# A two-expert feed-forward layer: the last batch's second layer by halves of the columns, its rows combined per half, and the sums of pieces on VectorE in that batch

## What is computed

```python
def _L0_ffn_ref(x, G, gate_w, up_w, down_w, lora_A, lora_B):   # x: the mask
    scores = softmax(einsum('bsh,he->bse', x, G))
    value, indices = top_k(scores, 2)
    w = einsum('bsk,bske->bse', value, onehot(indices))
    gate = silu(einsum('bsh,efh->bsef', x, gate_w))
    up = einsum('bsh,efh->bsef', x, up_w)
    out = einsum('bsef,bse,ehf->bsh', gate * up, w, down_w)
    lr = einsum('bsh,erh->bser', x, lora_A)
    return out + einsum('bser,bse,ehr->bsh', lr, w, lora_B)

return x + ffn
```

## Time and profile before

| | |
|---|---|
| median of 3 runs | 799.74 us (798.53 to 800.81) |
| the profiled execution: its own time | 801.34 us |
| the profiled execution: span from first to last instruction | 799.6 us |
| busy: TensorE matmul / VectorE / ScalarE / GpSimd | 500.2 / 518.0 / 450.5 / 386.0 us |
| chain that ended last: DMA / TensorE / VectorE / issue / GpSimd / ScalarE | 20 / 18 / 17 / 16 / 15 / 7% |
| moved by DMA | 147.29 MB, mean 184 GB/s |

### The profile page before, as it was taken

The page is one execution under the profiler, slowest core; times in us unless marked ns, Lnnn a source line. Parts: engine busy times, 40 slices in busy tenths (PEclk is TensorE's granted clock), DMA queues, the critical chain, the costliest instruction groups (busy, mean ns, idle before and its releaser), DMA issues.

```text
span 799.6 us, 13619 instructions
## 1 busy us (share of the span) xinstructions
PE 500.2 (63%) x3682; PEld 330.5 (41%) x3682; DVE 518.0 (65%) x1242; ACT 450.5 (56%) x655; POOL 386.0 (48%) x337
## 2 busy tenths in 40 slices
PE   0211187259878882687778716887779368888810
PEld 0210086136545551455445414554447155555500
DVE  5768789856697685776884867746872723233345
ACT  6687278837954576297446653875447245455410
POOL 7114200034365223387887224877973168768510
PEclk9755589668999995899999967989989779999965
DMA  9990060012312463368367823585479238758469
GB/s 317 360 270 0 4 260 27 1 40 98 128 71 103 146 238 102 119 227 287 132 222 227 349 94 130 181 274 183 158 251 361 86 107 293 248 179 283 174 259 381
DMA packets 76984, 147.29 MB, mean 184 GB/s; under 512 B 21475, under 2 KB 30699, under 8 KB 76400
## 3 DMA queue, kind: packets, MB, share of 16 engines
q1 hardware_dynamic: 59248, 104.40, 38.6%
q0 software_dynamic: 17664, 41.98, 14.3%
HBM read 95.47 MB, written 69.21 MB: 206 GB/s over the span
## 4 chain that ended last, share of the span: by engine, by line
DMA 20%; PE 18%; DVE 17%; issue 16%; POOL 15%; ACT 7%; DVEq 4%; SPq 3%; POOLq 1%; ACTq 0%
DMA piece<-put_rows 7%; DMA out_dram<-piece 6%; PE pa L692 6%; POOL piece L540 4%; ACT mask L807 3%; DMA xg<-mask_rows,where 3%; POOL piece L543 3%; DVE mask L1077 3%; POOL xg L523 2%; DMA w<-put_rows 2%; POOL put_rows L531 2%; DVE small L1039 1%; PE pc L718 1%; PE pc L715 1%; PE pc L717 1%
## 5 line engine op out<-in xcount | busy, mean ns | idle before, releaser
L692 PE MATMUL pa<-w,xt 128*128 x1472 | 204.1, 293 | 4.3 <-issue 4.2
L692 PEld LDWEIGHTS pa<-w,xt 128*128 128x128 f16 x1472 | 148.5, 101 | 67.2 <-issue 18.7
L864 ACT ACTIVATE y<-pc,where 128x512 f32<-128x512 f32 x184 | 125.5, 689 | 69.2 <-PE pc L718 69.0
L523 POOL DMA_INDIRECT xg<-mask_rows,where x92 | 97.2, 1056 | 119.4 <-DVEq L1351 93.8
L531 POOL DMA_INDIRECT put_rows<-y,where x92 | 92.4, 1005 | 127.7 <-ACT y L864 109.5
L1359 DVE SCALAR_TENSOR_TENSOR g_full<-pa,where,s_act 128x144 f32<-128x144 f32 x92 | 33.4, 364 | 176.3 <-ACT s_act L856 176.2
L851 ACT ACTIVATE xt<-pb 128x1024 f16<-128x1024 uint8 x92 | 94.1, 1023 | 92.4 <-PE pb L679 92.3
L856 ACT ACTIVATE s_act<-pa,small 128x128 f32<-128x128 f32 x92 | 33.9, 368 | 99.0 <-PE pa L692 99.0
L679 PE MATMUL pb<-ident,xg 128*128 128x128 f16 x368 | 38.6, 232 | 77.5 <-DMA xg<-mask_rows,where 59.1
L718 PE MATMUL pc<-lb,gt 128*128 x184 | 76.4, 415 | 0.0
L715 PE MATMUL pc<-wd,gt 128*128 x184 | 76.2, 414 | 0.3
(11 more groups left out here) (208 smaller groups left out, 863.4 us busy)
## 6 DMA issues: line engine op xcount, KB each, us to landing
piece<-put_rows SPq DMA_DIRECT2D x96, 256.0 KB, 3.9
v<-in_x_dram SPq DMA_DIRECT2D x40, 512.0 KB, 8.7
piece<-in_x_dram SPq DMA_DIRECT2D x48, 256.0 KB, 2.9
out_dram<-piece SPq DMA_DIRECT2D x48, 256.0 KB
w<-put_rows SPq DMA_DIRECT2D x16, 512.0 KB, 9.7
w<-in_L_ffn_gate_w_dram SPq DMA_DIRECT2D x8, 512.0 KB, 10.3
w<-in_L_ffn_up_w_dram SPq DMA_DIRECT2D x8, 512.0 KB, 8.3
wd<-in_L_ffn_down_w_dram SPq DMA_DIRECT2D x8, 512.0 KB, 9.5
```

The lines of the kernel that those rows point to most:

```text
L523: pool.indirect_dma_start(out=xg[:, g % NX, :], out_offset=None, in_=mask_rows[n % 2], in_offset=bass.IndirectOffsetOnAxis(ap=mask_row[n][ ...
L692: last = pe.matmul(l1[g % 2], xt[:, g % 2, t, :], w1[:, bass.ds(e, 1), t, k, :].rearrange("p o n -> p (o n)"), start=(t == 0 and k == 0), ...
L864: nc.scalar.activation(y[:, g % NY, half * HALF:(half + 1) * HALF], pc[:, half, :], ACT.Copy, scale=y_scale[n][:, i:i + 1]).then_inc(y_rea ...
```

## The change

In the last batch alone (`n == LAST`):

- The second layer runs by halves of the output columns. `half_layer(i, 0, e)` takes the place of `second_layer` in the loop over tiles; when the loop is over, `half_layer(i, 1, e)` runs for all 23 tiles, with the expert's number read again. So that the turned gates of all tiles stay, `store_gt` writes them to 23 buffers `late_gt`, 21 of them in the mask's memory and 2 in `gt`.
- ScalarE evicts a half as a unit of its own (`store_half`); the memory of `y` holds a ring of six halves. GpSimd puts each half (2 KB a row, up to 256 KB) with an indirect DMA of its own (`put_half`) into one of two new DRAM arrays `half_rows`: 46 puts in place of 23.
- SyncE waits for the puts of the first half, loads its 16 blocks of 256 KB, stores its 8 sums of 256 KB, and then does the same for the second half. VectorE adds by halves.
- The pieces of the batch before are added on VectorE, behind `store_gt` in the tile, and no longer on GpSimd.

Core of the diff:

```diff
+            def put_half(i, h):
+                u = late(h, i)
+                pool.wait_ge(y_ready, 2 * T * LAST + u + 1)
+                pool.indirect_dma_start(
+                    out=half_rows[h], out_offset=bass.IndirectOffsetOnAxis(ap=put_row[LAST][:, i:i + 1], axis=0),
+                    in_=late_y(u), in_offset=None,
+                    bounds_check=ROLES * S - 1, oob_is_err=False).then_inc(late_put[u % RING], 16)
...
-                    if i >= 3:
+                    if i >= 3 and n < LAST:
                         put_out(n, i - 3)
+                    elif i >= 3:
+                        put_half(i - 3, 0)
...
-                    if n > 0 and i in PIECE_AT:
+                    if 0 < n < LAST and i in PIECE_AT:
                         sum_piece(n - 1, PIECE_AT[i])
...
+            for i in range(T):
+                put_half(i, 1)
...
+            def half_layer(i, h, e):
+                u = late(h, i)
+                cols = slice(h * HALF, (h + 1) * HALF)
+                pe.wait_ge(gt_ready, tile(LAST, i) + 1)
+                pe.wait_ge(y_ready, 2 * T * LAST + u - 1)
...
+            for i in range(T):
+                half_layer(i, 1, load_expert(LAST, i))
...
+            def store_half(i, h):
+                u = late(h, i)
+                act.wait_ge(y_done, 2 * T * LAST + u + 1)
+                if u < RING:
+                    act.wait_ge(put[u // 2], 16 * len(range(u // 2, T * LAST, NY)))
+                else:
+                    act.wait_ge(late_put[u % RING], 16 * (u // RING))
...
+            def sum_piece(n, j):
+                u = PIECES * n + j
+                at = u % NC
+                dve.wait_ge(piece_landed[at], 48 * (u // NC + 1))
+                V.tensor_tensor(piece[:, at, 0, :], piece[:, at, 0, :], piece[:, at, 1, :], ALU.add)
+                dve.drain()
+                V.tensor_tensor(piece[:, at, 0, :], piece[:, at, 0, :], piece[:, at, 2, :],
+                                ALU.add).then_inc(summed_piece, 1)
...
+            for h in range(2):
+                cols = slice(h * HALF, (h + 1) * HALF)
+                for k in range(RING):
+                    sp.wait_ge(late_put[k], 16 * len(range(k, late(h, T), RING)))
+                for c in range(C):
+                    for r in range(ROLES):
+                        sp.dma_start(last_put[c][r][:, cols], half_roles[h][r][:, c, :]).then_inc(rows_landed[c], 16)
+                for c in range(C):
+                    sp.wait_ge(last_summed, C * h + c + 1)
+                    sp.dma_start(out_rows[n][:, c, cols], v[:, c, cols]).then_inc(last_stored, 16)
```

More of the change, by code:

```diff
@@ L214, in build @@
         expert_f = temp(T)
+        gt_cells = 3 * P
+        late_gt = [mask[:, k * gt_cells:(k + 1) * gt_cells].rearrange("p (t k) -> p t k", t=3)
+                   for k in range(NV // gt_cells)]
+        late_gt += [gt[:, i, :, :] for i in range(2)]
+        assert len(late_gt) >= T
         cells = [0]
@@ L306, in build @@
         put = [sem(f"put{i}") for i in range(NY)]
+        late_put = [sem(f"late_put{i}") for i in range(2 * NY)]
         piece_landed = [sem(f"piece_landed{i}") for i in range(NC)]
@@ L319, in build, with late, late_y @@
         out_rows = out.rearrange("b (p c) h -> b p c h", c=C)
+        half_rows = [nc.dram_tensor(f"half_rows{h}", [ROLES * S, HALF], F32, kind="Internal").ap()
+                     for h in range(2)]
+        half_roles = [a.rearrange("(r p c) h -> r p c h", r=ROLES, c=C) for a in half_rows]
+        LAST = B - 1
+        RING = 2 * NY
+        def late(half, i):
+            return T * half + i
+        def late_y(u):
+            return y[:, (u % RING) // 2, (u % 2) * HALF:(u % 2 + 1) * HALF]
         put_roles = [a.rearrange("(r p c) h -> r p c h", r=ROLES, c=C) for a in put_rows]
@@ L780, in _ @@
                     between(i, 2)
-                    if i >= 2:
+                    if i >= 2 and more:
                         second_layer(n, i - 2, experts[i - 2])
+                    elif i >= 2:
+                        half_layer(i - 2, 0, experts[i - 2])
                     between(i, 3)
@@ L940, in _ @@
                         exponential(n + 2, c)
+            for i in range(T - 2, T):
+                store_half(i, 0)
+            for i in range(T):
+                store_half(i, 1)
         @block.vector
@@ L1455, in _ @@
                     between(i, 2)
+                    if n == LAST and i in PIECE_AT:
+                        sum_piece(n - 1, PIECE_AT[i])
                 store_gt(n, T - 1)
```

71 lines of the change are left out of this document (44 added, 27 removed).

## The result

The changed kernel takes 814.62 us (median of 4 runs, 810.23 to 816.65) where the kernel before, on the same chip, takes 799.13 (4 runs, 794.29 to 800.81). The ratio is 1.0207, 95% interval 1.0167 to 1.0247: slower by 2.1%, where 0.9% was forecast and 814.0 was the range's upper end. The profiled execution took 815.52 us, its span is 813.8.

The account below looks back on a forecast made before the run. Last batch bound by waits in its 23-tile loop (piece cycle delaying gathers) and a transfer tail. Loop gains 12.5 us, puts cost 30.8, shorter tail gives 801.7, queueing adds 5.5: span 807.2, median 807.3 us; range 795 to 814.

Parts of the forecast that it names:

- The piece's cycle: Last batch's loop: store, load and sum of a piece in two buffers, forecast at 5.3 us a piece with sums on VectorE.
- A free tile: Loop tile without a piece: 3.97 us less 0.86 for four matmuls gives 3.1, taken as 3.2 us.
- The additions on VectorE: Piece sums moved from GpSimd: 0.62 us for each addition, 1.3 a piece with the drain.
- The puts: Second half on GpSimd: 23 more puts at 1.34 us, 30.8 us, plus 5.5 for the transfers beside them.
- How the queues share: First half's loads and stores beside second-half puts: puts get 105 GB/s, land in 5 to 9 us, lose 5.5 us.
- The tail: After the last put: 2.1 us landing, 3.0 latencies, 16.5 for the other 6.29 MB; some 21.6 us to the end.
- The sum: Whole span: last first-half put at 749.3, last put 780.1, end 801.7; with 5.5 us of queueing, 807.2 us.
- the even sharing: Rival for the second half: queues share evenly, puts stay 1.34 us apart beside loads, 801.7 us; chance 0.21.
- Faster pieces: Rival for the loop: piece stores land sooner, 4.6 us a piece, 800.2 us with queueing or 794.7 without; chance 0.18.
- TensorE does not pace the second half: Denies a rival: TensorE at the lower clock paces the second half, 8.3 us more on 801.7, or 812 to 815; chance 0.10.
- The hiding: Against it, a rival: first half's transfers outlast the second-half puts and delay its loads, up to 5 us; chance 0.03.

## Why the prediction was right and wrong

Right were the direction, and the reason for it: GpSimd's 23 further puts are the price, and what they hide is less. Wrong was the size: 807.3 forecast, 814.62 measured, 0.6 outside the range, because the loop was to gain 12.5 us and gained 4.4. The span was 6.6 over the forecast one. Step by step:

- *The piece's cycle* is the step that failed: "SyncE's queue alone needs 3.8 from store to load and 1.5 to issue the loads before it can turn to the next store, so I take 5.3." The form was right, since SyncE's queue is the whole cycle. The 3.8 was not: it came from one row of the kernel before, on the low side of its 3.6 to 4.7, and from a place where GpSimd's slower sum kept the store behind the loads by 0.5 us. In the changed kernel it is 4.66, and a piece 6.04. Each sum was later, and more so from one to the next: sum 3 by 1.4 us (669.02 for 667.6), sum 8 by 5.2 (699.20 for 694.0), sum 15 by 8.9 (745.30 for 736.4). Of these 8.9, the nine steps at the pace of the pieces make 7.0. (The 660.8 for sum 2 does not follow from the terms as they stand: 652 + 1.3 + 3.8 + 5.2 are 662.3, and 662.95 was measured.) With whole columns the same edit gives 6.5 a piece, and the kernel gets slower by it alone. A saving on the engine was counted while the transfer that it sets off was kept at its old duration.
- *A free tile.* I took 3.2 (3.1 by the matmuls) and it takes 3.75 with no piece in the way, 3.11 with the expert fixed. The missing 0.5 to 0.6 is the read of the expert's number. The prediction named that read as an unknown, but only for the second half ("TensorE reads the tile's expert number once more; no row shows what that costs"), where it indeed decides nothing. It did not see that the loop's own read had been covered by the four matmuls that it took away. In the changed kernel this decides little, since few of its tiles are free: from sum 8 to sum 11, where three tiles without a piece stand, only 0.5 us were lost. The last gate is 8.2 us late in all, 752.3 for 744.1.
- *The additions on VectorE*: 0.69 us each, 0.62 taken. It decides nothing.
- *The puts.* 30.8 + 5.5 = 36.3 forecast, 33.3 measured: 29.4 (1.28 apart, not 1.34) and 3.9 for the transfers beside them. By the sum the last put would be issued 36.3 behind the last first-half put, and this is the 3.0 that came back.
- *How the queues share.* Half puts land in 6.0 us beside the loads, as "5 to 9" said, and ScalarE waits for them up to 2.02. The software queue had 24.1% of the engines beside 36.2 for the other, then 31.5 beside 46.5 (772 to 795 us). The Trainium skill ("DMA: Bandwidth & Descriptors", section "Queues, rings and completion order") says that each engine takes turns among its queues by packets. The prediction read this as half the engines for the puts, and so as no cost; by the run with the transfers held the cost is 3.9 us. The two shares above are 40 to 60, neither half nor the 18.8 beside 81.6 of the earlier trace rows. But the two queues together held the engines for 60 and 78% of these stretches, so they did not both have work all the time, and the shares neither bear the rule out nor refute it.
- *The tail.* 22.6 from the last put, 21.6 forecast. 6.29 MB in 17.3 us (20.3 less 3.0 of latencies) are 364 GB/s, between the bounds of 350 and 411.
- *The sum*: +8.7 at the last first-half put (757.96 for 749.3), -3.0 for the puts, +1.0 for the tail: 6.6, with rounding. Had the puts cost what was forecast, the time would have been 3 us further out: the total is as near as it is because two errors had opposite signs.

Of the rivals, the even sharing did not come (3.9 us, not nil). Faster pieces came out the other way round: "the piece's own 768 KB of loads stay in front of the store", which stood against it, is what the rows show, and the store was later than in the kernel before. TensorE does not pace the second half: the granted clock is 1.00, that is 2.4 GHz, from 720 to 793, and GpSimd's 1.28 us are longer than TensorE's tile, although that took 1.16 in place of 0.86 (half layers at 757.34, 758.48, 759.66). The hiding works as said.

## What to carry to other kernels

Where a loop waits for a transfer, count the cycle of a buffer, not the work of the engine that sums it: the engine's share was 1.4 of 6 us, and making it faster moved the store closer to the loads and cost 4 us. With three more buffers the same edit gave 8.6, and buffers and edit together 11. When work is taken from an engine, look at what else this work was covering, here a read of a number behind four matmuls. And a split in two that doubles the number of indirect transfers costs the full issue time of each (1.28 us here with 2 KB rows, 1.31 with 4 KB rows); set it against what it hides before anything else: 31.1 against 12.9.

## What the runs showed of the hardware

- The read of a number by TensorE's sequencer leaves a gap of 0.3 to 0.5 us when four matmuls of 512 columns, or sixteen of 272, are issued ahead of it, and with eight of 512 a tile is only 0.04 us longer (4.01 for 3.97). The Trainium skill ("DMA: Bandwidth & Descriptors", section "Latency and other measured facts") gives a floor of about 600 ns for `tensor_load`. If this read is one, an estimate by that figure is that 0.86 us of matmuls would cover it, and these runs show that they don't.
- A store of 256 KB takes 4.1 to 6.2 us directly behind 768 KB of loads on the same DMA queue, 2.8 to 4.7 when it is issued 0.3 to 1.0 us behind them, 4.1 (median) on another engine's queue, and 2.0 with no load in flight. Half puts land in 2.7 us with no transfer beside them and in 6.0 with loads and stores (medians).
- The same 12.58 MB need 36.9 us from first load to end in 48 transfers with 2 KB rows and 33.65 in 24 with 4 KB rows; less 3.0 for latencies that is 371 GB/s against 411. The smaller ones ran at some 400 GB/s for most of the time too; what they lost lies in the first 5 us or so of each of the two blocks of loads, at 130 to 370 GB/s. The number of blocks differs as well as the size, so the cause is open.
